# Twelve tiles of each attention pass copied row by row through a DRAM strip, and another order of ScalarE's instructions at the step boundaries of layer 2

## The chip, the cores and the metric

The kernel runs on one core of one Trainium2 chip. A core has five engines with instruction queues of their own: TensorE (PE, matmul), VectorE (DVE), ScalarE (ACT), GpSimd (POOL) and SyncE (SP), and 16 DMA engines that all of them share. POOL issues indirect DMAs (gathers and scatters by an index tile); SP issues plain DMAs only, but an address of such a DMA can come from a register. The metric is the device time of one execution in microseconds; shorter is better.

## The reference

Four graph layers run over one graph of 3125 nodes and 103,125 edges, sorted by destination, each with a residual and a layer norm: a GIN layer (layer 0), a graph autoencoder of four attention layers (layer 1), a gated graph layer with five GRU steps (layer 2) and a relational layer (layer 3). The two that the change touches are:

```python
def _gat(x, src, dst, W, a_src, a_dst, b, concat, n):      # four times: C = 16, 32, 16, 64 channels, 8 heads
    h = (x @ W).reshape(n, H, C)
    e = leaky_relu((h * a_src).sum(-1)[src] + (h * a_dst).sum(-1)[dst], 0.2)
    ex = exp(e - segment_max(e, dst)[dst])
    alpha = ex / (segment_sum(ex, dst)[dst] + 1e-16)
    out = segment_sum(h[src] * alpha[:, :, None], dst)     # concatenated, or the mean over heads
    return out + b

for _ in range(5):                                         # layer 2
    h_all = einsum('nd,ted->nte', h, W) + b                # 4 edge types
    a = segment_sum(h_all[src, etypes], dst)
    h = gru(a, h)
```

## The kernel before, in words

**Attentions.** `gat` runs four times, as passes a (C = 16), b (C = 32), c (C = 16) and d (C = 64). A table `ht` in DRAM has one row of RW = 8C + 8 floats for each node. The 806 tiles of 128 edges are worked in NGR = 51 groups `GR` of KG = 16 tiles (the last has 6). For each tile, `gpsimd_pass` issues one indirect DMA (L1579) that gathers the 128 source rows into a slot of the ring `gbr` (RT = 48 slots, 32 in pass d). In passes a and c the last 2 or 3 tiles of a group, from group 16 in a and from group 4 in c, are not gathered but made by matmuls from node one-hots (`tensor_pick`, `scalar_pick`, `vector_hot`); passes b and d gather all 806 tiles. A slot is reused once TensorE has done the tile that it held (`tile_mm`).

Per group VectorE copies the scores out of the gathered rows (`vector_edge_scores`, L1390), after TensorE's transposes computes the logits (`vector_edge_logits`, to L1413), later multiplies the rows by the weights (`vector_edge_weights`, L1420 to L1432), makes the one-hots of the edge destinations (L1380) and counts edges for layer 2 (L350, passes a to c). TensorE multiplies each tile by its one-hot (L1543) and ScalarE adds up the PSUM planes (L1496, L1492 in d). TensorE turns the scores of the next group with L1522 and L1523, which wait for the copy L1390.

SyncE runs `sync_pass` beside that, once for every two groups: it waits for the logits of the group three back, loads the lists of two groups (L1614, L1615), in passes a to c waits for the edge counts of the group three back and broadcasts key rows (L1019), and in pass a also handles some slot rows (`sync_slot_rows`, L965 to L986).

After the last gather POOL scatters edge counts (L899) into `cnt_d`, which layer 2 reads; after pass d these scatters set when step 0 of layer 2 can go on.

**Layer 2.** Each of five steps multiplies counts from DRAM with a table of 25 node blocks, each as three bf16 parts: TensorE makes a block's row in PSUM (`tensor_row`, L2188, two banks in turn), ScalarE copies its high part (`scalar_row_high`, L2193), VectorE subtracts it (`vector_row_rest`, L2200), ScalarE copies the middle part (`scalar_row_mid`, L2206), and VectorE subtracts that as well (`vector_row_low`, L2211). Row b + 2 waits on TensorE for the rest of row b. Eight rows (AHEAD = 8) are made ahead of a step's end; rows 8 to 24 are made at its boundary, between which the last GRU gate of the step before stands (L2052 to L2064 on ScalarE, L2027 to L2041 on VectorE), and beside which TensorE works blocks 0 and 1 of the counts (L2259). The boundary ends with VectorE's clearing of the sum (L2357), the slot sums (L2322) and TensorE's merge (L2246).

**A row copy that exists already.** In layer 3, `sync_row_tiles` (L2134) has SyncE copy 12 tiles row by row: it loads 16 row numbers into registers at a time and issues one DMA of 256 bytes for each row, 1536 in all.

The waits are written by hand with counted semaphores; nothing is planned at run time.

Of the kernel before, what the change touches and what calls it, by code (L numbers as in the profile page):

```python
# [9 lines left out]
I32 = mybir.dt.int32  # L10
# [4 lines left out]
NB = 25  # L15
NP = NB * 128
# [5 lines left out]
NT = 806  # L22
# [11 lines left out]
KG = 16  # L34
GR = [(c, min(KG, NT - c)) for c in range(0, NT, KG)]
NGR = len(GR)
# [2 lines left out]
Q_A, Q_B = 31, 82  # L39
ROW_GROUPS = list(range(4, NG, 5))  # L40
NROW = len(ROW_GROUPS)


class Sig:
# [18 lines left out]
def build(nc, I, out):  # L63
    with ExitStack() as ctx:
        ctx.enter_context(nc.allow_non_contiguous_dma(reason="bias columns"))
        v, a, t, g, s = nc.vector, nc.scalar, nc.tensor, nc.gpsimd, nc.sync

        def sb(name, shape, dt=F32):
            return ctx.enter_context(nc.sbuf_tensor(name, shape, dt))
# [4 lines left out]
        def dsig(name):  # L74
            return Sig(ctx.enter_context(nc.semaphore(name)), 16)

        def dram(name, shape, dt=F32):
            return nc.dram_tensor(name, shape, dt).ap()
# [9 lines left out]
        ident = sb("ident", [128, 128])  # L88
        iota = sb("iota", [128, 128])
        ones = sb("ones", [1, 128])  # L90
        srcT = sb("srcT_s", [128, NT], I32)
        dstT = sb("dstT_s", [128, NT], I32)
        rel = sb("rel", [128, NT])
# [570 lines left out]
        def by_products(u):  # L664
            return FIRST <= u < NG
# [348 lines left out]
        def sync_count_rows(name, p):  # L1014

            if p >= 2:
                s.wait_ge(*mark["counts", name, 2 * p - 3])
            q = pair_quads(name, p)
            s.dma_start(count_rows[name][p % 2][:, 0:512 * len(q)],  # L1019
                        key_rows[512 * q[0]:512 * (q[-1] + 1)].partition_broadcast(128)).then_inc(*rows_in[p % 2].one())  # L1020
# [54 lines left out]
        def gat(name, kin, C, dst, following, bn):  # L1075
            HC = 8 * C
            RW = HC + 8
# [54 lines left out]
            def by_products(gi):  # L1132
                return PP if FIRST_G <= gi < NGR - 1 else 0

            def product_no(gi, j):
                return PP * (gi - FIRST_G) + j

            def product_tile(gi, j):
                return GR[gi][0] + KG - PP + j

            def gathered_of(gi):
                return 16 * sum(GR[x][1] - by_products(x) for x in range(gi % 3, gi + 1, 3))

            def vector_weights_stack():

# [238 lines left out]
            def vector_edge_scores(gi):  # L1384
                b, (c, n) = gi % 2, GR[gi]
                k = c % RT
                v.wait_ge(gat_g[gi % 3].sem, g0[gi % 3] + gathered_of(gi))
                if by_products(gi):
                    v.wait_ge(rows_put.sem, rp0 + product_no(gi + 1, 0))
                v.tensor_copy(sc[:, b, 0:8 * n].rearrange("p (k h) -> p k h", h=8),  # L1390
                              gbr[:, k:k + n, 0:8]).then_inc(*packed.one())

# [175 lines left out]
            def gpsimd_pass():  # L1568
                g.wait_ge(*tab.now())
                if PP:  # L1570
                    g.wait_ge(*mark["stacked" if name == "a" else "products", name])
                if layer == 0:
                    g.iota(quad_no, [[1, NQ]], base=0, channel_multiplier=0).then_inc(*quad_nos.one())
                for gi in range(NGR):
                    c0, n = GR[gi]
                    for c in range(c0, c0 + n - by_products(gi)):
                        if c >= RT and c % S == 0:
                            g.wait_ge(tile_mm.sem, tm0 + set_of(c - RT))
                        g.indirect_dma_start(  # L1579
                            out=gbr[:, c % RT, 0:RW], out_offset=None, in_=ht,  # L1580
                            in_offset=bass.IndirectOffsetOnAxis(ap=srcT[:, c:c + 1], axis=0)).then_inc(*gat_g[gi % 3].one())
                        if layer == 3:
                            scatter_counts(p0 + (p1 - p0) * c // NT, p0 + (p1 - p0) * (c + 1) // NT)
                s0 = p0 if layer < 3 else p1
                scatter_counts(s0, s0 + TAIL_)
                g.wait_ge(*tile_out.now())
                scatter_counts(s0 + TAIL_, s0 + TAIL_ + (BESIDE if layer < 3 else BESIDE_D))
# [15 lines left out]
            def sync_pass():  # L1603
                s.wait_ge(gat_sc.sem, sc0 + 16 * NB)
                s.wait_ge(*tab.now())
                if layer == 0:
                    for x in fseg_out:
                        s.wait_ge(*x.now())
                for gi in range(0, NGR, 2):
                    b, q, m, c = gi // 2 % 2, gi % 4, min(2, NGR - gi), GR[gi][0]  # L1610
                    n = sum(GR[gi + i][1] for i in range(m))
                    if gi >= 4:
                        s.wait_ge(logit.sem, lg0 + gi - 2)
                    s.dma_start(seg[:, q:q + m, :], seg_d[gi:gi + m].rearrange("g p c -> p g c")).then_inc(*lists_g[b].one())  # L1614
                    s.dma_start(sdl[:, q:q + m, :].rearrange("p b f -> p (b f)")[:, 0:8 * n],  # L1615
                                sdt_d[:, 8 * c:8 * (c + n)]).then_inc(*lists_g[b].one())
                    if layer == 0:
                        sync_slot_rows(gi)
                    if layer < 3:
                        sync_count_rows(name, gi // 2)  # L1620

            vector_table()
            scalar_table()
# [423 lines left out]
        def scalar_gate_rz(stp, i):  # L2047
            c, w = GATES[i]
            a.wait_ge(*gate2a.next())
            if (stp, i) != (0, 0):  # L2050
                a.wait_ge(*mark[before_gate(stp, i)])
            a.activation(r_[D:2 * D, 0:w], ps[4][D:2 * D, 0:w], ACT.Sigmoid, bias=brz[D:2 * D, 0:1]).then_inc(*A.one())  # L2052
            a.activation(z_[0:D, 0:w], ps[4][0:D, 0:w], ACT.Sigmoid, bias=brz[0:D, 1:2]).then_inc(*a2v.one())

        def scalar_gate_n(stp, i):
            c, w = GATES[i]
            a.wait_ge(*mark["rn", stp, i])
            a.activation(n_[0:D, 0:w], r_[0:D, 0:w], ACT.Tanh, bias=bih[0:D, 2:3]).then_inc(*a2v.one())

        def scalar_state(stp, i):  # L2060

            c, w = GATES[i]
            a.wait_ge(*mark["h", stp, i])
            a.activation(both[D:2 * D, c:c + w], xT[0:D, c:c + w], ACT.Copy).then_inc(*state.one())  # L2064
# [126 lines left out]
        def scalar_row_high(r0, b):  # L2191
            a.wait_ge(row_mm.sem, r0 + b + 1)
            a.activation(table[:, b, :, 0, :], ps[6 + b % 2][:, 0:256].rearrange("p (t f) -> p t f", f=D),  # L2193
                         ACT.Copy).then_inc(*row_high.one())
# [9 lines left out]
        def scalar_row_mid(r0, b):  # L2204
            a.wait_ge(row_rest.sem, r0 + b + 1)
            a.activation(table[:, b, :, 1, :], rest[b % 2].rearrange("p (t f) -> p t f", f=D),  # L2206
                         ACT.Copy).then_inc(*row_mid.one())
# [181 lines left out]
        def scalar_rows(r0, b0, b1):  # L2389
            for b in range(b0, b1):  # L2390
                scalar_row_high(r0, b)
                scalar_row_mid(r0, b)

        def scalar_step(stp):
            last, r0 = stp == 4, NB * stp
            if stp == 0:
                a.activation(both[D:2 * D, 0:NP], xT[0:D, :], ACT.Copy).then_inc(*state.one())
                scalar_rows(0, 0, AHEAD)
            scalar_rows(r0, AHEAD, AHEAD + 3)
            if stp:  # L2400
                scalar_gate_rz(stp - 1, NCOL - 1)
            scalar_rows(r0, AHEAD + 3, AHEAD + 4)
            if stp:
                scalar_gate_n(stp - 1, NCOL - 1)
            scalar_rows(r0, AHEAD + 4, AHEAD + 5)
            if stp:
                scalar_state(stp - 1, NCOL - 1)
            scalar_rows(r0, AHEAD + 5, NB)
            for i in range(NCOL - 2):
                scalar_gate_rz(stp, i)  # L2410
                scalar_gate_n(stp, i)
                if not last:
                    scalar_state(stp, i)
            scalar_gate_rz(stp, NCOL - 2)
            if last:
                scalar_gate_n(stp, NCOL - 2)
                scalar_gate_rz(stp, NCOL - 1)
                scalar_gate_n(stp, NCOL - 1)
            else:
                scalar_rows(r0 + NB, 0, 1)  # L2420
                scalar_row_high(r0 + NB, 1)
                scalar_gate_n(stp, NCOL - 2)
                scalar_row_mid(r0 + NB, 1)
                scalar_rows(r0 + NB, 2, 3)
                scalar_state(stp, NCOL - 2)
                scalar_rows(r0 + NB, 3, AHEAD)
# [142 lines left out]
```

## Time and profile before

| | |
|---|---|
| median of 3 runs | 8204.98 us (8196.1 to 8208.67) |
| profiled execution's own time | 8197.95 us |
| its span | 8196.7 us |
| busy share of PE, PEld, DVE, ACT, POOL | 70%, 64%, 57%, 28%, 64% |
| starts of the gathers L1579, first to last | a 1049.4 to 1981.2 us, b 2173.9 to 3182.4, c 3399.4 to 4247.9, d 4441.6 to 5458.0 |

Busy shares are means over stages with different limits. The idle column of a group of instructions names what the engine waited for last. An indirect DMA on POOL shows as some 0.94 us busy, followed by 0.30 us called "issue", in which POOL waits for nothing that the profile shows. SP's rows show when it issued a DMA and for how long; they are not counted as busy. PEclk or the last but two column of a windows row is the granted clock of TensorE as a share of 2.4 GHz.

### The profile page before, as it was taken

How to read it: one execution, taken by the hardware profiler on the slowest of the kernel's cores; microseconds unless marked ns; L12 is line 12 of the kernel's file. 1: busy time of each engine (PE TensorE's matmuls, PEld its weight loads, DVE VectorE, ACT ScalarE, POOL GpSimd, SP SyncE). 2: the span in 40 equal slices, each digit the busy share in tenths (PEclk: the TensorE clock that was granted, in tenths of full speed). 3: DMA queues.
4: the chain of work that ended last, by engine and by line, in shares of the span. 5: the costliest groups of instructions: out<-in, count | busy, mean ns of one | idle time of the engine just before them, and what ended most of it. 6: DMA issues, size and time to landing. Idle time of an engine off the chain costs nothing.

```text
span 8196.7 us, 138876 instructions
## 1 busy us (share of the span) xinstructions
PE 5763.4 (70%) x50188; PEld 5280.0 (64%) x50188; DVE 4654.4 (57%) x8857; ACT 2315.4 (28%) x6265; POOL 5284.6 (64%) x5497
## 2 busy tenths in 40 slices
PE   5888635887466666488876999979679999823333
PEld 3666535886366665377764888976669999723232
DVE  7777535776488887398884777763122222333333
ACT  0000023443134443044442666651011111112221
POOL 7777777777777776777777777777730000077776
PEclk9999767998588887599996999996889999966666
DMA  5554123332255552133323777753568988611111
GB/s 186 180 172 132 30 70 76 80 80 56 82 145 147 145 146 80 49 90 91 87 68 109 219 218 219 218 149 118 192 251 327 354 326 326 263 27 28 28 27 27
DMA packets 432169, 1151.54 MB, mean 140 GB/s; under 512 B 151749, under 2 KB 225350, under 8 KB 394168
## 3 DMA queue, kind: packets, MB, share of 16 engines
q0 software_dynamic: 225888, 471.27, 22.7%
q1 hardware_dynamic: 205596, 671.39, 22.6%
q8 instruction: 399, 6.54, 0.3%
q14 instruction: 286, 2.34, 0.1%
HBM read 1018.78 MB, written 120.93 MB: 139 GB/s over the span
## 4 chain that ended last, share of the span: by engine, by line
PE 35%; POOL 28%; issue 16%; DVE 12%; DMA 5%; ACT 2%; DVEq 1%; ACTq 0%; SPq 0%; POOLq 0%
POOL pool L1579 15%; PE ps L1543 11%; PE ps L2259 10%; POOL ACC L521 5%; POOL cnt_d L899 5%; PE ps L540 3%; PE ps L1224 3%; DVE ACC L496 2%; DMA pool<-d_h,srcT_s 2%; PE ps L1829 2%; POOL pool L521 2%; DVE pool L1432 2%; ACT ACC L1496 2%; DVE pool L1380 1%; POOL edge_d L1336 1%
## 5 line engine op out<-in xcount | busy, mean ns | idle before, releaser
L1543 PE MATMUL ps<-pool 128*106 128x128 f32 (+2 forms) x19344 | 2400.5, 283 | 50.9 <-DVE pool L1432 50.9
L1543 PEld LDWEIGHTS ps<-pool 128*106 128x106 f32 (+2 forms) x19344 | 2292.0, 170 | 61.2 <-DVE pool L1432 60.8
L1496 ACT ACTIVATE ACC<-ps 72x256 f32 (+1 forms) x2418 | 1010.4, 418 | 1485.2 <-PE ps L1543 1293.7
L521 POOL DMA_INDIRECT ACC<-t,ACC x410 | 386.9, 944 | 1245.7 <-DVE ps L2093 1121.0
L899 POOL DMA_INDIRECT cnt_d<-pool x806 | 842.8, 1046 | 317.3 <-issue 240.5
L1432 DVE TENSOR_TENSOR pool<-pool,ps 128x1024 f32<-128x1024 f32 (+1 forms) x807 | 927.4, 1209 | 0.0
L1579 POOL DMA_INDIRECT pool<-d_h,srcT_s x806 | 764.3, 948 | 245.5 <-issue 179.4
L1579 POOL DMA_INDIRECT pool<-b_h,srcT_s x806 | 764.2, 948 | 245.5 <-issue 231.2
L496 DVE TENSOR_TENSOR ACC<-ACC,ps 65x128 f32 (+1 forms) x1612 | 454.4, 282 | 809.9 <-PE ps L540 581.9
L1579 POOL DMA_INDIRECT pool<-a_h,srcT_s x738 | 708.1, 960 | 224.8 <-issue 215.9
L2259 PE MATMUL ps<-pool,ACC 128*128 128x192 bf16 x8600 | 767.8, 249 | 76.4 <-DMA ACC<-cnt_d 76.4
L2259 PEld LDWEIGHTS ps<-pool,ACC 128*128 128x128 f16 x8600 | 724.8, 99 | 113.3 <-issue 95.6
L1579 POOL DMA_INDIRECT pool<-c_h,srcT_s x668 | 631.2, 945 | 218.6 <-issue 182.6
L540 PE MATMUL ps<-pool 128*65 128x128 f32 (+1 forms) x2392 | 356.2, 313 | 455.0 <-issue 325.2
L1522 PE MATMUL ps<-ident,pool 128*128 128x128 f32 (+1 forms) x204 | 72.4, 355 | 845.5 <-DVE pool L1390 845.4
L540 PEld LDWEIGHTS ps<-pool 128*65 128x65 f32 (+1 forms) x2392 | 323.0, 162 | 482.0 <-issue 338.1
L521 POOL DMA_INDIRECT ACC<-i_x,srcT_s x505 | 502.5, 995 | 155.3 <-issue 153.0
L1522 PEld LDWEIGHTS ps<-ident,pool 128*128 128x128 f32 (+1 forms) x204 | 31.5, 154 | 883.8 <-issue 883.8
L1492 ACT ACTIVATE ACC<-ps 106x512 f32 x806 | 482.3, 598 | 369.5 <-PE ps L1543 358.8
L1390 DVE COPY pool<-pool 128x128 f32<-128x128 f32 (+1 forms) x204 | 49.1, 241 | 914.6 <-DMA pool<-a_h,srcT_s 291.9
L1380 DVE TENSOR_TENSOR pool<-ps,rel 128x1024 f32<-128x1024 f32 x404 | 485.8, 1213 | 0.0
L1224 PE MATMUL ps<-pool,ACC 128*96 128x128 f16 x6850 | 453.5, 229 | 40.8 <-ACT pool L1240 40.8
(346 smaller groups left out, 8856.2 us busy)
## 6 DMA issues: line engine op xcount, KB each, us to landing
ACC<-cnt_d SPq DMA_DIRECT2D x172, 1600.0 KB, 8.7
pool<-cnt_d SPq DMA_DIRECT2D x88, 1600.0 KB
cnt_d<-pool SPq DMA_DIRECT2D x26, 3200.0 KB
ACC<-t SPq DMA_DIRECT2D x1536, 0.2 KB
ACC<-key_d SPq DMA_DIRECT2D x17, 1280.0 KB
ACC<-key_d SPq DMA_DIRECT2D x21, 768.0 KB
ACC<-key_d SPq DMA_DIRECT2D x26, 512.0 KB
ACC<-key_d SPq DMA_DIRECT2D x13, 1024.0 KB
```

Source lines behind the costliest of these rows:

```text
L496: add = v.tensor_tensor(out=win, in0=win, in1=ps[bk][0:FA, 128 * i:128 * i + 128], op=ALU.add)
L521: g.indirect_dma_start(out=gb[b][:, k, :], out_offset=None, in_=table, in_offset=bass.IndirectOffsetOnAxis(ap=idx[:, c:c + 1], axis=0)).th ...
L540: mm = t.matmul(ps[u % banks][0:FA, 128 * i:128 * i + 128], msg[:, k0 + i, :], oh[b][:, k0 + i, :], start=True, stop=True)
L899: g.indirect_dma_start(out=cnt_d, out_offset=bass.IndirectOffsetOnAxis(ap=cidx[:, c:c + 1], axis=0), in_=cval[:, c:c + 1], in_offset=None) ...
L1224: mm = t.matmul(pick_out[:, 128 * h:128 * h + 128], x3[:, b, h, :, :].rearrange("p k f -> p (k f)"), hotT[j][:, b, :], start=(b == 0), sto ...
L1380: v.tensor_tensor(out=ohr[:, k:k + n, :], in0=count.unsqueeze(1).to_broadcast([128, n, 128]), in1=rel[:, c:c + n].unsqueeze(2).to_broadcas ...
L1432: product = v.tensor_tensor(out=gv, in0=gv, in1=wk[:, q:q + n_, :].unsqueeze(3).to_broadcast([128, n_, 8, C]), op=ALU.mult)
L1492: a.activation(win[:, 0:4, bass.ds(reg, 128)], pl[0].rearrange("p (i c) -> p i c", c=128), ACT.Copy)
L1496: a.activation(win[:, 0:NPL, bass.ds(reg, 128)], pl[0].rearrange("p (i c) -> p i c", c=128), ACT.Copy).then_inc(*(tile_out if last else A) ...
L1543: mm = t.matmul(o, gbr[:, tile % RT, M * i:M * i + M], oh, start=True, stop=True)
L1579: g.indirect_dma_start(out=gbr[:, c % RT, 0:RW], out_offset=None, in_=ht, in_offset=bass.IndirectOffsetOnAxis(ap=srcT[:, c:c + 1], axis=0) ...
L2259: mm = t.matmul(ps[b % 2][:, 0:192], ring[u % NR][:, i, :], table[:, sb_, q, :, :].rearrange("p k f -> p (k f)"), start=(j == 0), stop=(j ...
```

## The change

A list `STAGED` of 12 groups (4, 8, ... 48) is added. In each of the four passes the first tile of such a group is no longer gathered by POOL. SyncE instead reads its 128 source numbers (`srcR1`, a new input laid out on the host) into the tile `ones`, 64 at a time in two halves, loads them into registers by 16, and copies each row with one DMA from `ht` to a DRAM strip `staged`. 64 such copies stand at the end of each of the first 24 turns of SyncE's loop. When it comes to the staged group itself, SyncE waits for the 128 copies of its strip and for the slot, and loads the strip into the ring with one DMA; VectorE waits for this one (`tile_put`) beside the gathers.

In layer 2 the ScalarE order at the boundary is changed: the high part of row b + 1 is copied before the middle part of row b. The gate's first activations (`scalar_gate_rz`) stand ahead of the high part of row 11, the tanh after the middle part of row 10, the copy of the state after that of row 12. TensorE's and VectorE's orders stay.

```diff
+STAGED = list(range(4, NGR - 1, 4))
...
+        row_nos = [ones[0:1, 64 * j:64 * j + 64].bitcast(I32) for j in range(2)]
+        nos_in = [dsig("row_numbers0_in"), dsig("row_numbers1_in")]
...
+            staged = dram(name + "_staged", (len(STAGED), 128, RW))
+            rows_staged = [dsig(name + "_staged0"), dsig(name + "_staged1")]
+            tile_put = dsig(name + "_tile_put")
+            n0 = [x.sent for x in nos_in]
+
+            def sync_row_numbers(part):
+                if part < 2 * len(STAGED):
+                    s.dma_start(row_nos[part % 2], I["srcR1"][:, 64 * part:64 * part + 64]).then_inc(*nos_in[part % 2].one())
+
+            def sync_stage_rows(part):
+
+                i, h = part // 2, part % 2
+                if i >= len(STAGED):
+                    return
+                s.wait_ge(nos_in[h].sem, n0[h] + 16 * (i + 1))
+                for e0 in range(0, 64, 16):
+                    _, regs = nc.values_load_multi_w_load_instructions(
+                        row_nos[h][0:1, e0:e0 + 16], engines=[mybir.EngineType.SP], min_val=0, max_val=NP - 1,
+                        skip_runtime_bounds_check_because="sources are node numbers")
+                    for e in range(16):
+                        p = 64 * h + e0 + e
+                        s.dma_start(staged[i, p:p + 1, :], ht[bass.ds(regs[e], 1), :]).then_inc(*rows_staged[i % 2].one())
+                sync_row_numbers(part + 2)
+
+            def sync_staged_tile(gi):
+
+                i, c = STAGED.index(gi), GR[gi][0]
+                s.wait_ge(rows_staged[i % 2].sem, 16 * 128 * (i // 2 + 1))
+                if c >= RT:
+                    s.wait_ge(tile_mm.sem, tm0 + set_of(c - RT))
+                s.dma_start(gbr[:, c % RT, 0:RW], staged[i]).then_inc(*tile_put.one())
+
             def gathered_of(gi):
-                return 16 * sum(GR[x][1] - by_products(x) for x in range(gi % 3, gi + 1, 3))
+                return 16 * sum(GR[x][1] - by_products(x) - (x in STAGED) for x in range(gi % 3, gi + 1, 3))
...
+                if gi in STAGED:
+                    v.wait_ge(tile_put.sem, 16 * (STAGED.index(gi) + 1))
...
-                        if c >= RT and c % S == 0:
+                        if c == c0 and gi in STAGED:
+                            continue
+                        if c >= RT and (c % S == 0 or (c == c0 + 1 and gi in STAGED)):
                             g.wait_ge(tile_mm.sem, tm0 + set_of(c - RT))
...
+                sync_row_numbers(0)
+                sync_row_numbers(1)
                 for gi in range(0, NGR, 2):
...
+                    if gi in STAGED:
+                        sync_staged_tile(gi)
+                    sync_stage_rows(gi // 2)
...
-            scalar_rows(r0, AHEAD, AHEAD + 3)
-            if stp:
-                scalar_gate_rz(stp - 1, NCOL - 1)
-            scalar_rows(r0, AHEAD + 3, AHEAD + 4)
-            if stp:
-                scalar_gate_n(stp - 1, NCOL - 1)
-            scalar_rows(r0, AHEAD + 4, AHEAD + 5)
-            if stp:
-                scalar_state(stp - 1, NCOL - 1)
-            scalar_rows(r0, AHEAD + 5, NB)
+            scalar_row_high(r0, AHEAD)
+            for b in range(AHEAD, NB):
+                if stp and b == AHEAD + 2:
+                    scalar_gate_rz(stp - 1, NCOL - 1)
+                if b + 1 < NB:
+                    scalar_row_high(r0, b + 1)
+                scalar_row_mid(r0, b)
+                if stp and b == AHEAD + 2:
+                    scalar_gate_n(stp - 1, NCOL - 1)
+                if stp and b == AHEAD + 4:
+                    scalar_state(stp - 1, NCOL - 1)
...
+    arr["srcR1"] = pad(a["src"], NT * 128).reshape(NT, 128)[[KG * gi for gi in STAGED]].reshape(1, 128 * len(STAGED))
```

## Rows read from the trace of the kernel before

**Rows 1.** Windows, one inside each attention pass: us, busy by engine, PEclk, DMA share, GB/s

```profile
1100.00:1900.00 800.00, 574.00 (x6182) 564.15 (x6180) 531.97 (x969) 301.86 (x849) 607.48 (x632) 0.88 0.32 78
2250.00:3100.00 850.00, 560.39 (x4211) 552.77 (x4212) 681.37 (x1471) 339.42 (x715) 643.15 (x680) 0.83 0.51 147
3450.00:4200.00 750.00, 605.76 (x6560) 569.20 (x6559) 649.47 (x1025) 326.63 (x998) 556.08 (x590) 0.95 0.33 89
4500.00:5400.00 900.00, 820.51 (x7316) 804.21 (x7315) 637.29 (x892) 554.07 (x1472) 681.27 (x719) 1.00 0.78 219
```

**Rows 2.** The gather's line, by pass: duration ns min/median/max, first and last start us

```profile
L1579 POOL DMA_INDIRECT pool<-b_h,srcT_s x806: 942/946/1066, 2173.9 to 3182.4; - x162
L1579 POOL DMA_INDIRECT pool<-d_h,srcT_s x806: 942/946/1122, 4441.6 to 5458.0; - x162
L1579 POOL DMA_INDIRECT pool<-a_h,srcT_s x738: 940/944/5460, 1049.4 to 1981.2; - x185
L1579 POOL DMA_INDIRECT pool<-c_h,srcT_s x668: 938/944/1048, 3399.4 to 4247.9; - x167
```

**Rows 3.** Waits of VectorE in the four windows: us in total, times, longest

```profile
DVE pool L1390 <- DMA pool<-a_h,srcT_s: 225.1, 41, 11.0
...
DVE pool L1390 <- DMA pool<-b_h,srcT_s: 159.3, 43, 5.4
...
DVE pool L1390 <- ACT pool L1240: 59.9, 41, 2.0
...
DVE pool L1390 <- DMA pool<-d_h,srcT_s: 222.8, 45, 6.4
```

**Rows 4.** Waits of POOL in c's window and of TensorE in d's

```profile
POOL pool L1579 <- PE ps L1543: 33.0, 61, 2.0
...
PE ps L1522 <- DVE pool L1390: 38.6, 40, 2.2
```

**Rows 5.** Layer 3: its row copies on SP, and gathers beside them (7200 to 7900)

```profile
L2134 SPq DMA_DIRECT2D ACC<-t x1536: 224/225/319, 7169.0 to 7932.0; - x192
...
L521 POOL DMA_INDIRECT pool<-t,ACC x282: 940/944/953, 7204.8 to 7875.3; - x141
```

**Rows 6.** Timeline of SP: a one-row DMA of 16 KB, then one turn in c

```profile
1244.48 0.24 SPq L976 DMA_DIRECT2D slot_d<-ACC  x1
...
3749.36 0.37 SPq L1614 DMA_DIRECT2D pool<-seg_d  x1
...
3771.30 0.32 SPq L1019 DMA_DIRECT2D ACC<-key_d  x1
3783.51 0.37 SPq L1614 DMA_DIRECT2D pool<-seg_d  x1
```

**Rows 7.** Windows over the four boundaries of layer 2, columns as in rows 1

```profile
6076.50:6112.70 36.20, 32.61 (x292) 27.91 (x290) 21.38 (x51) 14.62 (x39) 0.00 (x0) 0.95 0.62 249
6331.00:6367.20 36.20, 32.29 (x246) 26.57 (x243) 20.77 (x50) 15.64 (x41) 0.00 (x0) 0.86 0.38 143
6590.00:6626.20 36.20, 32.04 (x261) 26.70 (x260) 20.96 (x50) 15.49 (x41) 0.00 (x0) 0.91 0.43 161
6847.50:6883.70 36.20, 32.61 (x268) 27.41 (x266) 20.98 (x50) 15.40 (x41) 0.00 (x0) 0.91 0.44 167
```

**Rows 8.** Timeline of TensorE at the second boundary: start, us, idle before

```profile
6339.38 0.70 PE L2188 MATMUL ps<-pool 65*128 65x256 f32 x2 [0.81 <-DVE pool L2200]
...
6342.43 0.70 PE L2188 MATMUL ps<-pool 65*128 65x256 f32 x2 [1.68 <-DVE pool L2200]
...
6344.36 1.22 PE L2188 MATMUL ps<-pool 65*128 65x256 f32 x2 [0.35 <-DVE pool L2200]
...
6367.23 0.43 PE L2246 MATMUL ps<-pool 128*64 128x128 f32 x2 [0.62 <-DVE pool L2322]
```

**Rows 9.** Timeline of ScalarE there

```profile
6342.85 0.52 ACT L2064 ACTIVATE ACC<-pool 64x384 f32<-64x384 f32 x1
6343.39 0.38 ACT L2193 ACTIVATE pool<-ps 128x256 bf16<-128x256 f32 x1
```

## Prediction, written before the changed kernel ran

> **What bounds the kernel now.** I read the windows inside the four attention passes first, then the gather's line, then who VectorE, POOL and TensorE waited for there, then SyncE's timeline, and last the timeline of a boundary of layer 2.
>
> The windows show no engine near full by its busy column in passes a and b: POOL is busy 607 of 800 us in a and 643 of 850 us in b [rows 1]. But a gather shows 0.94 us busy and the starts are further apart: in b 806 gathers start from 2173.9 to 3182.4, which is 1008.5 us / 805 = 1.253 us each [rows 2]. In d it is 1016.4 / 805 = 1.263 us with seven other scatters between. So POOL is filled from the first gather to the last, and VectorE's copy of the scores waits for the gathered rows in nearly every group: 225 us in 41 waits in a's window, 159 us in b's, 223 us in d's [rows 3]. Passes a, b and d are bound by the number of gathers times 1.25 us.
>
> Pass c is another case. Its gathers are 668, or 835 us at 1.25, against 848.5 us from first to last [rows 2]. POOL itself waits for slots there, 33.0 us in 61 waits of up to 2.0 us [rows 4], and what VectorE waits for in its steady part is ScalarE's copy of the tiles made by matmul (59.9 us) [rows 3]. VectorE is busy 649 of 750 us [rows 1]. Pass c is bound by the loop of VectorE, TensorE and ScalarE, with POOL just below it.
>
> At a boundary of layer 2 TensorE has its matmuls ready but waits for the chain high part, rest, middle part, low part of the table rows, and for the gate between them: 0.81, 1.68 and 0.35 us for rests and 0.62 us for the slot sum at the end [rows 8]. Right behind the second of these waits the granted clock falls: a row's two matmuls take 1.22 instead of 0.70 us [rows 8], and the mean clocks of the four boundaries are 0.95, 0.86, 0.91 and 0.91 [rows 7].
>
> **The change, part by part.**
>
> *Gathers removed.* 12 in each pass. In a, b and d a removed gather takes 1.25 us off the chain: 12 x 1.25 = 15.0 us a pass, 45 us in three. What is late next? In a VectorE has 225/41 = 5.5 us of waiting a group and in b 159/43 = 3.7 us [rows 3]; a staged group is only 1.25 us shorter, so POOL stays the bound. In d TensorE is busy 820.5 of 900 us and waits 38.6 us in 40 waits for the copy of the scores [rows 1, 4]; the 41 us that are left are other short waits, which stay. That second wait, about 0.97 us a group, is the room: 3.9 us over four groups, against 1.25 us taken. It suffices. For a, b and d the bounds are 0 (the time turns into another wait at once) and 15 us each; I take 15, since in all three the waits are larger than the saving.
>
> In c the loop of the other engines stays. Only the first staged group falls where the gathers may still be late (the first groups have no tiles made by matmul). I take 1 us; bounds 0 and, if all of POOL's time counted, 15.
>
> What follows a pass (POOL's scatters after it, then the tables) starts with the last groups and moves forward as a whole; this holds after d too, where the scatters feed layer 2.
>
> *Row copies added on SyncE.* This is the unknown. The nearest row is layer 3's copy: 1536 DMAs start from 7169.0 to 7932.0, 0.497 us each, of which the DMA instruction itself is 0.225 us [rows 5]. The new copies have the same register source, but rows of 544, 1056 or 2080 bytes and a DRAM target. A one-row DMA of 16 KB was issued in 0.24 us [rows 6], so size alone adds little: 0.497 to 0.515 us a row. A turn of SyncE's loop is then 64 x 0.497 = 31.8 us, plus 0.37 and 0.47 for the lists, 0.32 for the key row, some 0.25 for the next numbers and 0.37 / 2 for the strip's load: 33.4 us (the second list load by the nearest row, L1614, and a tenth more for its shorter pieces). A turn may last two groups. In b and d these are 32 x 1.25 = 40 us, in a's later part 28 x 1.25 = 35 us, and in c one turn went from 3749.36 to 3783.51, 34.1 us [rows 6]. So SyncE fits everywhere, in c by 0.7 us, in a (34.4 us then) by 1.0. If the copies take 0.515 us, a turn is 34.6 us and slips by 0.5 us in c, 12 us over 24 turns. Against that stands its lead: the copies follow the wait for the counts of three groups back, the next lists go out 32 us later, and they are wanted about one group later still, so about 16 us of slip costs nothing. I cost it at nothing; what it costs if it is slower is a rival below.
>
> Queued behind SyncE's new wait for the strip's slot (`tile_mm`) are the next row copies and, behind them, the lists of the next turn; for these TensorE waits (L1522). In a to c SyncE has by then waited for edge counts that come later than that matmul, so the wait is free. In d there are no counts, and the slot's matmul comes about a group after the logits that started the turn, 16 x 1.25 = 20 us and some more, say 26. With 33 us of copies behind it the next turn starts some 19 us after its logits instead of with them; its lists are wanted about two groups, 40 us, after these. No cost, and the turn after it has no such wait and makes the delay good. The strip's load is a DMA of 128 rows, like one gather, issued about a group before it is wanted.
>
> *DMA load.* The staged tiles are moved twice more: 12 of 806, 3% more bytes. Beside layer 3's row copies the gathers went at their usual pace, 0.944 us median [rows 5]. The most loaded pass is d with a DMA share of 0.78 [rows 1]. Cost 0, bound +10 us in d.
>
> The Trainium skill (DMA: Bandwidth & Descriptors, Issuing engines are not separate DMA queues) says that DMAs issued from different engines run on the same 16 DMA engines, and that issuing from several only saves the sequencer's time, usually small against the DMA. By this rule the move to SyncE would bring next to nothing. The trace speaks against it as the limit here: the DMA engines are busy 32%, 51% and 78% in a, b and d while POOL has no gap [rows 1].
>
> *Boundaries of layer 2.* ScalarE now has the high part of the next row out before it waits for the rest of this one. Following rows 8 and 9: the gate's first activations start about 0.85 us earlier, since the middle part of row 10 no longer stands ahead of them; so the rest of row 11 is done before TensorE wants its row, and the wait of 0.81 us goes. The tanh and the gate's last three VectorE instructions start some 1.4 us earlier, but TensorE arrives 0.8 us earlier too: of 1.68 us about 1.3 stay. The high part of row 13 was copied at 6343.39, behind the middle part and the state (0.42 + 0.52 us) [rows 9]; now it stands ahead of both, and the wait of 0.35 us goes. At the end the last rows are done some 0.4 us earlier, which comes off the 0.62 us. Sum: 0.8 + 0.4 + 0.35 + 0.4 = 2 us a boundary, 8 us for four. The fallen clock costs (1 - 0.95) x 36.2 = 1.8 us at the first boundary, and 5.1, 3.3 and 3.3 us at the others, 13.5 us together [rows 7]. TensorE still waits once for over a microsecond, so I count about a third back, 5 us. Sum 13 us; bounds: 2 us (only the end wait) and 22 us (all of the clock).
>
> *Sum.* 45 + 1 + 13 = 59 us. The profiled execution took 8197.95 us, which gives 8139; it lies 7.0 us under the median of 8204.98, so against the median 8146 us.
>
> **Rivals.**
>
> *SyncE becomes the bound (slower).* Place: the row copies in c and a. It decides from a price of about 0.52 us a row, only 5% above that of layer 3. At 0.55 us a turn is 64 x 0.55 + 1.6 = 36.8 us: in c 2.7 us too long, over 23 turns 62 us, less 16 of lead = +46; in a 1.8 x 17 = 31, less 16 = +15 instead of -15; b and d gain their 15 each and layer 2 its 13: +46 + 15 - 30 - 13 = +18, 8223 us. At 0.60 us it would be a turn of 40 us and some +170 us. For it: a DRAM target is a form that no row shows. Against: the one-row store of 16 KB at 0.24 us.
>
> *Half of it.* Pass d gives nothing, because its DMA engines (0.78) or TensorE (0.91) take over as soon as POOL is early, and the clock of layer 2 falls as before: 30 + 8 = 38 us less the 3 us that the strips and c may cost, 35 us, 8170 us. For it: TensorE's small room in d. Against: rows 4.
>
> *Only layer 2 gains.* The gathers are limited by their DMAs, as the skill's rule above has it, or SyncE just holds the pace of POOL: 13 us or less, 8195 us. Against: the gather's constant 1.25 us in all four passes, with rows of 544 to 2080 bytes.
>
> **How the numbers follow.** Forecast 62%, half of it 18%, only layer 2 6%, SyncE the bound 14% (three quarters of it above 8205). About 0.2%, 16 us, is what can be told from no change. The forecast's own spread is 8125 (all of the clock and some of c) to 8165. The range: from 8125 to 8192, which holds the forecast, the half and little of the others. Faster by more than 0.2% (below 8189): forecast and half, and a few per cent of the rest, 0.83. Within: 0.06. Slower: 0.11.
>
> **What would show it.** Right: a first-to-last span of gathers 15 us shorter in a, b and d and nearly the same in c; VectorE's waits for gathers still there in a, b and d; SyncE's turns in c at the loop's length, with some idle left; a row copy at 0.50 us; the waits of 0.81 and 0.35 us gone at each boundary. Wrong: list loads L1614 on whose arrival TensorE's L1522 waits; a row DMA of clearly over 0.24 us; VectorE waiting for the strip; passes a or c longer than before.

## The result

The changed kernel takes 10736.06 us (median of 4 runs, 10731.73 to 10737.57) against 8205.95 us: a ratio of 1.3092, 95% interval 1.3072 to 1.3111. It is 2530 us slower. The forecast was 8146 us with a range to 8192. The direction was wrong, and the price of the rival "SyncE becomes the bound" (18 us more, at 0.55 us a row) was too small by a factor of over 100.

The chain of waits of the changed kernel names the place at once (shares of the span, first by engine, then by line):

```profile
SPq 51%; PE 16%; issue 15%; POOL 10%; DVE 4%; DMA 2%; DVEq 1%; ACT 0%; ACTq 0%; POOLq 0%
SPq L1165 44%; PE ps L2303 8%; SPq L1160 5%; POOL ACC L524 4%; POOL cnt_d L902 4%; PE ps L543 2%; DVE ACC L499 2%; PE ps L1873 2%; POOL pool L524 1%; POOL edge_d L1371 1%; PE ps L1580 1%; PE ps L1861 1%; DVEq L482 1%; DVE pool L532 1%; PE ps L1850 1%
```

L1165 is the row copy and L1160 the load of its numbers into registers. SyncE, which had 0% of the chain before, now carries half of the span. The row copy's line answers to L2134 of [rows 5] (duration ns min/median/max, first and last start):

```profile
L1165 SPq DMA_DIRECT2D a_staged<-a_h x1536: 609/627/1409, 1056.9 to 2532.2; - x192
L1165 SPq DMA_DIRECT2D b_staged<-b_h x1536: 701/729/1299, 2756.6 to 4384.0; - x192
L1165 SPq DMA_DIRECT2D c_staged<-c_h x1536: 609/627/1454, 4635.7 to 6103.4; - x192
L1165 SPq DMA_DIRECT2D d_staged<-d_h x1536: 731/758/1753, 6319.1 to 7987.4; - x192
```

The instruction takes 0.63 to 0.76 us, not 0.225. What follows from it is seen in SyncE's timeline in pass c, which answers to [rows 6] (start, us, line):

```profile
4941.87 57.88 SPq L1165 DMA_DIRECT2D c_staged<-c_h  x64
4999.81 0.41 SPq L1151 DMA_DIRECT2D ones<-i_srcR  x1
5000.27 0.39 SPq L1655 DMA_DIRECT2D pool<-seg_d  x1
5000.70 0.46 SPq L1656 DMA_DIRECT2D pool<-edge_d  x1
5001.21 0.43 SPq L1022 DMA_DIRECT2D ACC<-key_d  x1
5001.74 0.37 SPq L1174 DMA_DIRECT2D pool<-c_staged  x1
5003.50 26.46 SPq L1165 DMA_DIRECT2D c_staged<-c_h  x29
```

A turn of SyncE's loop lasts 5003.50 - 4941.87 = 61.6 us, without any wait in it, where two groups took 34.1 us before. (The blank of 1.4 us ahead of the last row is the load of row numbers into registers, L1160, which this list leaves out.) The lists (L1655, L1656) and the key row (L1022) leave only behind 64 copies. The median turns in a, b, c and d are 61.6, 67.9, 61.5 and 69.7 us. The waits of VectorE and TensorE in pass a (window 1100 to 2500) say who stands still for that:

```profile
DVE pool L1427 <- DMA pool<-a_staged: 403.1, 11, 45.8
DVE pool L1427 <- DMA pool<-a_h,srcT_s: 30.2, 4, 10.9
...
PE ps L1559 <- DMA pool<-edge_d: 353.7, 12, 40.5
```

Every second turn VectorE waits for the strip (up to 45.8 us), in the others TensorE waits for the list (up to 40.5 us); the wait for gathers, 225 us in [rows 3], has shrunk to 30. The gathers' line answers to [rows 2]:

```profile
L1618 POOL DMA_INDIRECT pool<-b_h,srcT_s x794: 940/947/1128, 2752.4 to 4403.9; - x199
L1618 POOL DMA_INDIRECT pool<-d_h,srcT_s x794: 940/947/1079, 6314.9 to 8012.3; - x199
L1618 POOL DMA_INDIRECT pool<-a_h,srcT_s x726: 938/945/5489, 1051.7 to 2550.6; - x182
L1618 POOL DMA_INDIRECT pool<-c_h,srcT_s x656: 938/945/1121, 4631.5 to 6120.2; - x164
```

From first to last start: a 1498.9 us (931.8 before), b 1651.5 (1008.5), c 1488.7 (848.5), d 1697.4 (1016.4): +567, +643, +640, +681, together +2531 us. A gather itself is as long as before; POOL is waiting for free slots (the gathers waited 2761 us in all for TensorE's matmuls, 125 us before). Of the two traces, which lie 2537 us apart, the stretches around and between the passes add some 24 us more, and layer 2 takes 19 off.

The mean granted clock falls as well (0.73, 0.69, 0.76 and 0.78 inside the four passes, 0.88, 0.83, 0.95 and 1.00 in [rows 1]). That comes with TensorE's waits of up to 40 us and is not the cause: SyncE's turn holds no wait for TensorE or any other engine.

Layer 2 went the other way. At its boundaries only one wait for a rest is left (timeline of TensorE in the changed kernel, answering to [rows 8]):

```profile
8894.82 0.70 PE L2232 MATMUL ps<-pool 65*128 65x256 f32 x2 [1.04 <-DVE pool L2244]
8914.07 0.43 PE L2290 MATMUL ps<-pool 128*64 128x128 f32 x2 [0.37 <-DVE pool L2366]
```

### The profile page after: what moved, and what is told of

The parts are those of the page before. It is cut to its first block, busy times and chain, and to the rows that moved or that the text cites. A ratio compares the mean times of both kernels' runs of the same rounds, so it can differ in the third digit from the quotient of the medians.

```text
span 10733.3 us, 157863 instructions
## 1 busy us (share of the span) xinstructions
PE 5790.8 (54%) x50188; PEld 5321.1 (50%) x50188; DVE 4652.4 (43%) x8857; ACT 2316.5 (22%) x6265; POOL 5248.0 (49%) x5449
## 4 chain that ended last, share of the span: by engine, by line
SPq 51%; PE 16%; issue 15%; POOL 10%; DVE 4%; DMA 2%; DVEq 1%; ACT 0%; ACTq 0%; POOLq 0%
SPq L1165 44%; PE ps L2303 8%; SPq L1160 5%; POOL ACC L524 4%; POOL cnt_d L902 4%; PE ps L543 2%; DVE ACC L499 2%; PE ps L1873 2%; POOL pool L524 1%; POOL edge_d L1371 1%; PE ps L1580 1%; PE ps L1861 1%; DVEq L482 1%; DVE pool L532 1%; PE ps L1850 1%
## 5 line engine op out<-in xcount | busy, mean ns | idle before, releaser
L1580 PE MATMUL ps<-pool 128*106 128x128 f32 (+2 forms) x19344 | 2424.9, 285 | 29.9 <-DVE pool L1469 29.9
L1580 PEld LDWEIGHTS ps<-pool 128*106 128x106 f32 (+2 forms) x19344 | 2319.2, 171 | 36.9 <-DVE pool L1469 35.4
L1437 DVE TENSOR_TENSOR_SCAN pool<-pool,small,ps 128x128 f32<-128x128 f32 (+1 forms) x204 | 96.6, 474 | 1406.9 <-PE ps L1560 1398.1
```

Source lines behind the costliest of these rows:

```text
L1580: mm = t.matmul(o, gbr[:, tile % RT, M * i:M * i + M], oh, start=True, stop=True)
```

## The experiments

Where a kernel leaves out or changes part of the work, the text or its expectation says so. Times are medians; ratios are to the kernel before on the same chip. Theory: the row copy is dear because of what it copies from and to, and SyncE's turn then no longer fits into two groups. Rivals: its number, the gathers beside it, or the pieces alone are to blame.

**Layer 2's order alone.** The kernel before with the last hunk of the ScalarE order.

> The kernel before with only ScalarE's new order at the boundaries of layer 2. In the changed kernel's trace one step of layer 2 repeats every 251.9 us, before it was 257.5 and 257.0. Theory 'the order does it': four boundaries at 5.3 us, so 8205 - 21 = 8184 us, with the waits of 0.81 and 0.35 us gone and less of the boundary at the low clock. Rival 'the steps are shorter only because of something the slow passes left behind' (counts in place earlier, another clock phase): 8195 to 8205 us.

Measured: 8185.53 us, ratio 0.9977 (0.9968 to 0.9986), 19 us less. Windows over its four boundaries, columns as in [rows 7]:

```profile
6082.00:6118.20 36.20, 34.32 (x323) 29.81 (x322) 22.90 (x56) 16.40 (x45) 0.00 (x0) 1.00 0.72 292
6336.65:6372.85 36.20, 34.31 (x325) 29.68 (x323) 21.71 (x53) 14.89 (x41) 0.00 (x0) 1.00 0.57 221
6591.00:6627.20 36.20, 34.79 (x340) 30.79 (x340) 20.32 (x50) 13.62 (x37) 0.00 (x0) 1.00 0.61 243
6844.00:6880.20 36.20, 34.79 (x347) 31.01 (x345) 20.17 (x48) 13.10 (x36) 0.00 (x0) 1.00 0.61 246
```

The granted clock stays at its upper level, 2.4 GHz, at all four, where it was 0.95, 0.86, 0.91 and 0.91 of it. From the merge ahead of a boundary's rows to the one behind them TensorE takes 27.4 us at each, where it took 30.7, 34.4, 32.9 and 32.4: 21.0 us less together, 13.5 of them the clock's. This half of the change works by itself.

**The gate later.** High parts first, but the gate's first activations behind row 10's middle part. In the new order that is one high part later than before the change.

```diff
-                if stp and b == AHEAD + 2:
-                    scalar_gate_rz(stp - 1, NCOL - 1)
                 if b + 1 < NB:
                     scalar_row_high(r0, b + 1)
                 scalar_row_mid(r0, b)
                 if stp and b == AHEAD + 2:
+                    scalar_gate_rz(stp - 1, NCOL - 1)
+                if stp and b == AHEAD + 3:
                     scalar_gate_n(stp - 1, NCOL - 1)
```

> The kernel before with high parts first at the boundaries of layer 2, but the gate's first activations behind the middle part of row 10 (as before the change, and so behind the high part of row 11 too), the tanh behind the middle part of row 11. Theory 'the gate's place decides': the gate starts later than before, the waits for the rests of rows 11 and 12 stay or grow, the clock falls as before, and little is left of the 19 us: 8195 to 8210 us. Rival 'high parts first is what counts': 8186 us again and no low clock at the boundaries.

Measured: 8203.93 us, ratio 1.0002 (0.9993 to 1.0012): nothing is left. Its waits for rests sum to 35.9 us in 24, those of the run before this one to 20.3 us in 20, those of the kernel before the change to 34.4 us in 28 (line L2188, who it waited for):

```profile
  DVE pool L2200: 35.9, 24
```

The profiled execution took 8189.45 us and so lies under the median, but not because of layer 2: from its first to its last merge layer 2 takes 1389.1 us in this trace, 1389.5 in that of the kernel before and 1370.3 with the new order. At the second boundary TensorE waits 1.77 us for one rest and 0.86 us for the next, and a row takes 1.1 to 1.2 us again:

```profile
6338.09 1.22 PE L2188 MATMUL ps<-pool 65*128 65x256 f32 x2 [0.86 <-DVE pool L2200]
...
6340.39 1.11 PE L2188 MATMUL ps<-pool 65*128 65x256 f32 x2
```

The mean clock from merge to merge is 0.89, 0.89, 0.89 and 0.90. High parts first are worth nothing while the gate starts late. An early gate without high parts first was not run, so what the early gate is worth by itself stays open.

**The gathers left out.** No copies, no strips, and their waits taken out; 12 gathers less.

```diff
-                if gi in STAGED:
-                    v.wait_ge(tile_put.sem, 16 * (STAGED.index(gi) + 1))
...
-                    if gi in STAGED:
-                        sync_staged_tile(gi)
-                    sync_stage_rows(gi // 2)
```

> The changed kernel with all row copies, strips and the waits for them taken out: the 12 tiles a pass are not gathered and nothing is put in their place (the slot keeps old rows). It shows what 12 gathers less are worth by themselves. Theory 'POOL's gathers bound a, b and d': first to last gather 15 us shorter in a, b and d and about 1 us in c, time 8205 - 46 - 21 = 8138 us. Rival 'another engine takes over at once': d or b keep their length, 8155 to 8184 us.

Measured: 8139.33 us, ratio 0.9925 (0.9910 to 0.9940). From first to last gather 916.9 us in a, 994.3 in b, 856.8 in c and 1001.6 in d: 14.9, 14.2 and 14.8 us less in a, b and d. In c it is 8 us more, but the run with layer 2's order alone has 856.5 us there too, without any tile left out; that is the spread of pass c and no effect. The benefit that was forecast for the attentions (46 us) exists.

**The strip in SBUF.** The same rows, the same number of copies, beside the same gathers; the target is one partition of an SBUF strip.

```diff
-            staged = dram(name + "_staged", (len(STAGED), 128, RW))
+            NSTRIP = 1 if C == 64 else 2
+            strip = [ns128[:, 270 * j:270 * j + RW] for j in range(NSTRIP)]
...
+                if h == 0 and i >= NSTRIP:
+                    s.wait_ge(tile_put.sem, 16 * (i - NSTRIP + 1))
...
-                        s.dma_start(staged[i, p:p + 1, :], ht[bass.ds(regs[e], 1), :])
+                        s.dma_start(strip[i % NSTRIP][p:p + 1, :], ht[bass.ds(regs[e], 1), :])
```

> The whole change, but each row is copied into a strip in SBUF (one partition a row) and the strip from there into the ring; two strips, one in pass d. Theory 'the copy is slow because it goes from DRAM to DRAM, where it is cut in pieces or waits for the target': a row costs 0.50 us again as in layer 3, instead of 0.90 to 1.06, a turn of SyncE some 33.5 us, and the time is 8205 - 46 - 21 = 8138 us if that turn fits in every pass. Rival 'a turn of 33.5 us is already too long': passes a, b and d gain 15 us each, c gets longer by some 10 to 20 us and VectorE waits for the strip there, 8150 to 8165 us. Rival 'the rows cost what they cost because of their number and the gathers beside them': still 0.9 us a row and about 10,500 us.

Measured: 8141.89 us, ratio 0.9927 (0.9912 to 0.9942). It beats both kernels, the one before by some 60 us and the changed one by 2594 us, and lies 4 us under the forecast of 8146. Its row copies in a and d, and a turn in c:

```profile
L1169 SPq DMA_DIRECT2D ns<-a_h x1536: 224/227/311, 1052.9 to 1918.7; - x192
...
L1169 SPq DMA_DIRECT2D ns<-d_h x1536: 224/228/307, 4424.2 to 5359.4; - x192
```

```profile
3721.21 30.61 SPq L1169 DMA_DIRECT2D ns<-c_h  x64
3751.87 0.24 SPq L1153 DMA_DIRECT2D ones<-i_srcR  x1
...
3754.93 30.42 SPq L1169 DMA_DIRECT2D ns<-c_h  x64
```

0.227 and 0.228 us an instruction, whether the row has 544 or 2080 bytes, and a turn of 33.7 us (33.4 forecast). So neither the number of copies nor the gathers beside them were to blame. A layer 3 copy takes 0.225 us in every run of this document, so instruction times can be compared between runs on different chips.

**One piece a row.** Is it the pieces? Rows of 131, 263 and 509 floats, still from DRAM to DRAM.

```diff
+            CW = {16: 131, 32: 263, 64: 509}[C]
-                        s.dma_start(staged[i, p:p + 1, :], ht[bass.ds(regs[e], 1), :])
+                        s.dma_start(staged[i, p:p + 1, :], ht[bass.ds(regs[e], 1), 0:CW])
```

> The changed kernel with rows copied from DRAM to DRAM as there, but only 131 of 136, 263 of 264 and 509 of 520 floats of each (the last 5, 1 or 11 are left as they were in the slot). These counts are prime. The packets of the changed kernel are 68, 88 and 160 bytes, that is 8, 12 and 13 pieces a row. Theory 'pieces': a prime count can't be cut, one packet a row, the DMA instruction is back at 0.23 us, a row at 0.50 us, and the time at 8140 to 8165 us. Rival 'DRAM target': the instruction still takes 0.6 to 0.76 us and the time stays near 10,700 us.

Measured: 9910.9 us (one run), and one packet a row in the trace, of 524, 1052 and 2036 bytes. The rival was right: the instruction still takes

```profile
L1166 SPq DMA_DIRECT2D a_staged<-a_h x1536: 538/556/742, 1057.5 to 2419.9; - x192
```

and the same in b, c and d. The pieces are the smaller part, 0.07 us of 0.40 in a.

**More piece counts.** `CW = {"a": 134, "b": 262, "c": 128, "d": 508}`.

> The changed kernel with row lengths of 134, 262, 128 and 508 floats in passes a, b, c and d (what is beyond them is left as it was in the slot). So far, all with DRAM as target: one piece a row takes 0.556 us of SyncE's DMA instruction whatever its length (131, 263 or 509 floats), 8 pieces 0.627, 12 pieces 0.729, 13 pieces 0.758 us. Theory 'a base of some 0.55 us and a little for each piece': 2 pieces in a and b (0.56 to 0.58 us), 16 pieces of 32 bytes in c (0.76 to 0.85 us), 4 in d (0.57 to 0.60 us). Rival 'bytes of a packet count too' (13 pieces of 160 bytes against 12 of 88): c below 0.73 us. The time of the whole lies near 10,100 us, since c's rows are slow and the others fast.

Measured: 9880.94 us (one run). 2 pieces 0.565 us, 4 pieces (of 508 bytes) 0.587 us, as the theory had it; but 16 pieces, expected as the dearest, are the cheapest:

```profile
L1166 SPq DMA_DIRECT2D c_staged<-c_h x1536: 492/492/1797, 4289.0 to 5521.9; - x192
```

Both theories missed this, and the runs don't say why.

**One DRAM tensor.** The strip as extra rows of the table's tensor `hts`, lengths as in the run with one piece a row.

```diff
-                        s.dma_start(staged[i, p:p + 1, :], ht[bass.ds(regs[e], 1), 0:CW])
+                        s.dma_start(hts[NP + 128 * i + p:NP + 128 * i + p + 1, 0:CW], ht[bass.ds(regs[e], 1), 0:CW])
```

> As the run with prime row lengths (131, 263, 509 floats, the rest of the row left as it was), but the strip is made of extra rows of the same DRAM tensor as the table. Theory 'two DRAM tensors in one instruction': the instruction takes its addresses through a table of tensors, and a jump between two entries costs the extra 0.33 us; with one tensor the instruction is back at 0.23 us, a row at 0.50 us, the time at 8140 us. Rival 'DRAM to DRAM as such': 0.556 us stays and the time is again 9910 us.

Measured: 10116.24 us (one run), 0.584 to 0.589 us an instruction, not less than 0.556. The jump between two tensors isn't the cause.

**Two sources, SBUF strip.** Every odd row from `I["x"]`.

> The kernel with the strip in SBUF, but every odd row of a strip is read from another DRAM tensor (64 floats of the input x; the rest of such a row is left as it was). One DRAM address an instruction, as there, but the tensor changes with each. Theory 'changing between tensors costs': the instruction rises from 0.225 us to 0.39 or 0.55 us for each row, and the time to 9000 us or more. Rival 'DRAM to DRAM as such': 0.225 us stays, 8142 us.

Measured: 8153.73 us (one run), 0.225 to 0.228 us an instruction for either source. This says the same from the other side.

**A constant source row.** `ht[p:p + 1, 0:CW]` in place of the register's row.

> As the run with prime row lengths, DRAM to DRAM, but the source row is a constant one instead of one from a register (the copied rows are the wrong ones). Theory 'the register matters': the instruction falls well below 0.556 us. Theory 'DRAM to DRAM' or 'two tensors': 0.556 us stays; the move and the register operation before each DMA go (0.07 us), so a row takes about 0.76 instead of 0.83 us and the time is near 9600 us.

Measured: 8284.69 us (one run), and 0.517 us an instruction: only 0.04 us belongs to the register. A row came to 0.56 us here, not 0.76. The loads of the numbers, of which the expectation had not thought, went as well (1.5 us for 16 rows), and that is about half of the difference. The kernel is also a point on the curve of the rival: with turns of 38.2 us in a and c it is 71 us over the kernel before on the same chip (8214.08, one run), a being 24 us longer and c 88 us.

**A row from SBUF to DRAM.** `rel[p:p + 1, 0:CW]` as the source.

> As the run with constant source rows and prime lengths (DMA instruction 0.517 us, DRAM to DRAM), but the source row is one of the SBUF tile rel, so that each copy goes from SBUF to DRAM (what is copied has nothing to do with the table). Theory 'it takes DRAM on both sides': the instruction falls to 0.22 to 0.25 us, a turn to some 18 us, and the time is that of the run without staged gathers, 8140 us. Rival 'a DRAM target is enough': 0.517 us stays, 8285 us.

Measured: 8147.07 us (one run).

```profile
L1166 SPq DMA_DIRECT2D a_staged<-rel x1536: 212/252/427, 1056.3 to 1905.1; - x192
```

0.252 us, and the same in b, c and d. A DRAM target alone costs next to nothing, and so does a DRAM source alone (0.227); it takes DRAM on both sides.

**Half the rows.** The DRAM strip and whole rows, but 6 tiles a pass: `STAGED = list(range(8, NGR - 1, 8))`, 32 rows a turn.

> The changed kernel, DRAM strip and whole rows as there, but only 6 tiles a pass (every eighth group), so that SyncE copies 32 rows a turn instead of 64. Theory 'a turn of SyncE must fit into two groups': 32 rows at 0.90, 1.00, 0.90 and 1.06 us make turns of 31 to 37 us, against 35 to 40 us of two groups in a, b and d and 34 us in c; so nothing is lost, 6 gathers of 1.25 us are saved in a, b and d, and the time is 8205 - 22 - 19 = 8164 us. Rival 'rows from DRAM to DRAM also slow the gathers or the strips': still over 8205 us, halfway to 10,736.

Measured: 8161.01 us, ratio 0.9955 (0.9939 to 0.9972). The instruction is as dear as in the changed kernel, and nothing of it is seen in the time. A turn in c:

```profile
3722.37 0.46 SPq L1656 DMA_DIRECT2D pool<-edge_d  x1
3726.15 0.32 SPq L1022 DMA_DIRECT2D ACC<-key_d  x1
3727.88 28.70 SPq L1165 DMA_DIRECT2D c_staged<-c_h  x32
```

Between the list and the key row SyncE waits 3.3 us for VectorE again (21 such waits in c, 58.5 us), which it did not do once in c with 64 rows. The length of SyncE's turn against two groups is the whole mechanism.

**Not in c.** The SBUF strip, with `STAGED = []` in pass c.

> The kernel with the strip in SBUF, but pass c gathers all its tiles as before. Theory 'c is bound by VectorE, TensorE and ScalarE': the same time as with it, 8142 us, and c from first to last gather as long as before. Rival 'the 12 gathers in c were worth their 15 us': 8155 us. Rival 'SyncE's turn of 33.7 us was holding c back': 8135 us or less.

Measured: 8142.28 us, ratio 0.9933 (0.9916 to 0.9949), c 848.3 us from first to last gather. The theory held: c's 1536 copies bring nothing that could be told from the spread.

## Why the prediction was wrong

*What bounds the kernel* was right: a, b and d by POOL, c by the others. The run without the 12 gathers and that without staging in c show both.

*Gathers removed*, 46 us: right in size (14.9, 14.2 and 14.8 us for 15, 15 and 15; nothing to be told from spread in c for 1).

*Row copies on SyncE*, 0.497 to 0.515 us each, cost 0: this is the step that failed. A copy took 57.88 / 64 = 0.90 us in c and 1.04 in d, and by that SyncE's turn of 61.5 to 69.7 us, forecast at 33.4, became the bound of all four passes. The price came from layer 3's copy, which has SBUF as target, and the bound from a store from SBUF. Each had one DRAM side, and I took a DRAM target for the only new thing, when what was new was DRAM on both sides. That is worth 0.556 - 0.225 = 0.33 us; the rest, 0.07 in a and c, 0.17 in b, 0.20 in d, comes with 8, 12 and 13 pieces a row, though not by their number alone, as 16 pieces were the cheapest. I had bounded the unseen form by two rows that agreed with each other; the range of 0.497 to 0.515 was no bound.

The Trainium skill (DMA: Bandwidth & Descriptors, Why a DMA increments its semaphore by 16 and not by 1) says that a DMA issued by SyncE runs on k engines, the largest k up to 16 that divides the slowest dimension of both sides, and that software can split a contiguous row for this. The trace agrees for the copies from DRAM to DRAM: rows of 136, 264 and 520 floats went in 8, 12 and 13 pieces. The packets of SyncE's queue show it, in the changed kernel and in the one with the strip in SBUF (packets, MB, share):

```profile
q1 hardware_dynamic: 338652, 684.64, 18.4%
q1 hardware_dynamic: 224988, 684.41, 23.4%
```

The difference of 113,664 is 2 x 1536 x (7 + 11 + 7 + 12), two packets for each piece beyond the first. With the strip in SBUF no row is split: the run with prime lengths has the same 224,988. The page gives no price for a piece.

*Turn of SyncE*: the sum of 33.4 us was right for the price put in (33.7 us in c with the SBUF strip), and so was the point of decision. The signs named for being wrong are all there: a row DMA of over 0.24 us, TensorE waiting for a list, VectorE waiting for the strip, a and c longer. Only the size of the rival was wrong: it was worked out for 0.55 and 0.60 us. Past that point the slack of 16 us is gone after one turn and every turn costs in full: 24 turns of 61.6 us are 1479 us, against 1488.7 us from first to last gather in c. The forecast gave this mechanism a chance of 14% and worked it out no further than some +170 us.

*DMA load*, 0: right, the gathers keep 0.946 us.

*Boundaries of layer 2*, 13 us: the mechanism was right and its size too small, with 19 us measured. The order gave 1.9 us at the second boundary, as forecast: from merge to merge it was 34.38 us, of which 5.1 belong to the clock, and is 27.36. The clock term was mis-sized: I counted 5 of 13.5 us back, and all 13.5 came back. The waits of 0.81, 1.68 and 0.35 us had shrunk to one of 1.04, and with waits of 1.77 and 0.86 us, in the run with the gate later, the low clock was there again.

## What to carry to other kernels

Price an instruction by a row that has both its operands in the same memories; a row copy from DRAM to DRAM issued on SyncE is not the one to SBUF with another target. When work is moved to an idle queue, sum that queue's whole turn and compare it with the period of the loop that waits for it: below it the work cost nothing here, even at 0.9 to 1.04 us a row, above it every microsecond counts in every turn, so a forecast near that edge needs a range that reaches far over it. A strip between two DMAs belongs in SBUF where 0.5 to 2 KB a partition can be found, here in a buffer dead since the preparation.

## What the hardware showed that I had not expected

- SyncE's DMA instruction for one row: 0.225 us DRAM to SBUF (with 256 to 2080 bytes), 0.252 us SBUF to DRAM, 0.556 us DRAM to DRAM in one piece, from 524 to 2036 bytes. With more pieces it took 0.565 (2), 0.587 (4), 0.627 (8), 0.729 (12) and 0.758 us (13), and only 0.492 us with 16. Why two DRAM sides cost 0.33 us stays open; a jump between tensors isn't it, and the register is only 0.04 us of it.
- Waits of 0.81 and 1.68 us, one row apart (with a third of 0.35 or 0.57 us at two of the boundaries), were followed by some 3 to 10 us at 1.2 GHz at each of four boundaries, a wait of 1.04 us by none at any of four.
